# A graph network on one core: how the second layer norm takes its variance, is scaled, turned and stored

## What is computed

```python
# x: 50000 x 64; W: 8 relations x 64 x 64; rel: the relation of each edge
xw = jnp.einsum('ni,rih->rnh', x, W)
transformed = xw[rel, src]
x = _layernorm(x + segment_sum(transformed, dst, 50000))

def _layernorm(x, axis=-1, eps=1e-05):
    m = jnp.mean(x, axis=axis, keepdims=True)
    v = jnp.var(x, axis=axis, keepdims=True)
    return (x - m) / jnp.sqrt(v + eps)
```

## Time and profile before

| | |
|---|---|
| median of 3 runs | 4799.02 us (4790.83 to 4802.06) |
| the profiled execution | 4836.87 us, its span 4835.2 us |
| TensorE matmul busy | 3475.6 us, 72% of the span |
| GpSimd (POOL) busy | 2850.0 us, 59% |
| VectorE (DVE) busy | 2155.2 us, 45% |
| ScalarE (ACT) busy | 1390.9 us, 29% |
| mean granted TensorE clock | 0.703 |
| DMA | 589.50 MB, mean 122 GB/s over the span |

### The profile page before, as it was taken

How to read it: one execution, slowest core, us unless ns; L and a number is a source line. 1 busy time by engine, 2 the same in 40 slices (tenths; PEclk the granted TensorE clock), 3 DMA queues, 4 the chain that set the end, 5 groups by cost and what they waited for, 6 DMA issues and landing times. The chain is left out here.

```text
span 4835.2 us, 72365 instructions
## 1 busy us (share of the span) xinstructions
PE 3475.6 (72%) x19803; PEld 2837.2 (59%) x19803; DVE 2155.2 (45%) x5433; ACT 1390.9 (29%) x3272; POOL 2850.0 (59%) x2834
## 2 busy tenths in 40 slices
PE   4665537766777537776677998779977777777778
PEld 3342127766333236675577667767746677766778
DVE  8999923342899412223322223424542222622225
ACT  1110002222455401112222564434432222222235
POOL 1778867775677767775577660001127776277753
PEclk9776755555799855555688999989985555755559
DMA  4002312112688731112665785545652111311115
GB/s 132 3 3 80 125 32 55 53 48 76 225 330 329 265 128 27 27 27 98 227 178 153 250 255 174 184 167 203 233 193 86 27 27 25 125 27 27 27 39 185
DMA packets 311487, 589.50 MB, mean 122 GB/s; under 512 B 178785, under 2 KB 180702, under 8 KB 292960
## 3 DMA queue, kind: packets, MB, share of 16 engines
q1 hardware_dynamic: 146819, 465.93, 27.1%
q0 software_dynamic: 87808, 66.01, 6.6%
q10 hardware_dynamic: 76506, 53.12, 3.4%
HBM read 286.68 MB, written 310.95 MB: 124 GB/s over the span
## 5 line engine op out<-in xcount | busy, mean ns | idle before, releaser
L1286 PE MATMUL e_ring<-e_msgs,e_hot 128*128 x6272 | 1387.7, 422 | 574.7 <-DVEq L1158 574.7
L1286 PEld LDWEIGHTS e_ring<-e_msgs,e_hot 128*128 128x128 f32 x6272 | 1352.1, 332 | 611.9 <-issue 611.9
L1035 POOL DMA_INDIRECT e_msgs<-y,index_D x784 | 740.0, 944 | 341.1 <-issue 220.9
L1150 DVE TENSOR_TENSOR e_hot<-e_nodes,keys_D 128x2048 f32<-128x2048 f32 x147 | 336.8, 2291 | 1107.3 <-SPq L1074 1087.0
L611 POOL DMA_INDIRECT list_S<-s_place,s_target x392 | 439.8, 1122 | 216.2 <-issue 119.2
L611 POOL DMA_INDIRECT list_D<-d_place,d_target x392 | 385.5, 983 | 161.5 <-issue 119.0
L1593 POOL DMA_INDIRECT m_far<-x,index_S x392 | 382.5, 976 | 154.1 <-issue 114.3
L1035 POOL DMA_INDIRECT e_msgs<-y,index_S x392 | 386.8, 987 | 135.3 <-issue 117.4
L1035 POOL DMA_INDIRECT e_msgs<-x_by_relation,index_D x392 | 373.0, 951 | 134.7 <-issue 109.1
L2441 POOL TENSOR_TENSOR n_sq<-n_cent 128x1792 f32<-128x1792 f32 x14 | 44.4, 3173 | 671.9 <-DVE n_cent L2336 671.9
L1384 ACT ACTIVATE rows_late<-e_ring,dinv 128x64 f32<-128x64 f32 x784 | 171.5, 330 | 757.0 <-PE e_ring L1286 757.0
(11 more groups left out here) (395 smaller groups left out, 5453.9 us busy)
## 6 DMA issues: line engine op xcount, KB each, us to landing
x_by_relation<-d_stage SPq DMA_DIRECT2D x98, 1024.0 KB, 5.3
m_keyrow<-keys_by_step SPq DMA_DIRECT2D x49, 512.0 KB, 4.6
rows<-pairs_by_edge SPq DMA_DIRECT2D x49, 512.0 KB, 4.7
messages<-rows SPq DMA_DIRECT2D x98, 256.0 KB
rows<-messages SPq DMA_DIRECT2D x49, 512.0 KB, 4.2
sums<-m_stage ACTq DMA_DIRECT2D x98, 256.0 KB, 3.6
n_in<-sums SPq DMA_DIRECT2D x14, 1792.0 KB, 8.2
s_xc<-x_padded SPq DMA_DIRECT2D x28, 448.0 KB, 3.7
```

The source lines that it names most:

```text
L1035: pool.indirect_dma_start(out=msgs[:, (i % HELD) * D:(i % HELD + 1) * D], out_offset=None, in_=source, in_offset=bass.IndirectOffsetOnAxis ...
L1150: nc.vector.tensor_tensor(hot[g % 2][:, :, :], bc(nodes[:, 0:P].unsqueeze(1), [P, GS, P]), bc(order["keys"][:, g * GS:(g + 1) * GS].unsque ...
L1286: mm = nc.tensor.matmul(ring[:, bass.ds(bucket, D)], hot[g % 2][:, k, :], msgs[:, bass.ds(tile, D)], start=False, stop=False, skip_group_c ...
```

## The change

Only the part of `stair_pass` under `normed` changes, that is pass `e1`.

- The sums of squares are taken bank by bank while the edges are still being added: after ScalarE has copied bank m out and refilled the ring, it runs eight `Square` activations of 128x64, each with `accum_out` into one column of `var`, now 128x392. The squares themselves go to `blank` and are not read. VectorE's reductions are gone.
- Behind the last bank there is one root over 128x392 on ScalarE and one reciprocal over 128x392 on VectorE.
- The scaling goes bank by bank: banks m with m % 5 of 0 or 2 (20 of them) on POOL, the other 29 on VectorE.
- TensorE turns a whole bank (four transposes) at a time into one of three PSUM banks; ScalarE alone copies them out, 512 values at a time, into `flat_t`, now a ring of 16 banks in `msgs`.
- SP stores groups of four banks (1 MB), in 13 groups: `x2` when the four banks are scaled, then `x2_turned` when they are turned. The last group has one bank.

```diff
+            def by_pool(m):
+                return m % 5 in (0, 2)
+
+            def wait_normed(eng, count):
+                eng.wait_ge(s_norm_pool, sum(by_pool(m) for m in range(count)))
+                if count > 1:
+                    eng.wait_ge(s_norm_dve, sum(not by_pool(m) for m in range(count)))
+
+            def normalize(on, m):
+                return on.tensor_tensor(of_nodes(bank(m)), of_nodes(bank(m)),
+                                        bc(rstd[:, m * BL:(m + 1) * BL].unsqueeze(2), [P, BL, D]), ALU.mult)
+
+            def flat_t(m, count=1):
+                return msgs[:, m % (TBUFS * TBANKS) * 512:(m % (TBUFS * TBANKS) + count) * 512]
...
@@ POOL
             if normed is not None:
-                for c in range(CHUNKS):
-                    pool.wait_ge(s_rstd, c + 1)
-                    nc.gpsimd.tensor_tensor(nodes_of(rows[:, c * CW:(c + 1) * CW]), nodes_of(rows[:, c * CW:(c + 1) * CW]),
-                                            bc(rstd[c % 2][:, :].unsqueeze(2), [P, CH, D]), ALU.mult
-                                            ).then_inc(s_norm, 1)
+                pool.wait_ge(s_rstd, 1)
+                for m in range(BANKS):
+                    if by_pool(m):
+                        normalize(nc.gpsimd, m).then_inc(s_norm_pool, 1)
...
@@ SP
+                starts = range(0, BANKS, TBANKS)
+                for n, m in enumerate(starts):
+                    count = min(TBANKS, BANKS - m)
+                    wait_normed(sp, m + count)
+                    sp.dma_start(x_out[:, m * 512:(m + count) * 512], bank(m, count)).then_inc(s_xout, 16)
+                    sp.wait_ge(s_turn, m + count)
+                    sp.dma_start(x_turned[:, m * 512:(m + count) * 512], flat_t(m, count)).then_inc(s_tout[n % TBUFS], 16)
+                sp.wait_ge(s_xout, 16 * len(starts))
+                for h in range(TBUFS):
+                    sp.wait_ge(s_tout[h], 16 * len(starts[h::TBUFS]))
...
@@ VectorE
+                dve.wait_ge(s_std, 1)
+                nc.vector.reciprocal(rstd[:, :], std[:, :]).then_inc(s_rstd, 1)
+                dve.wait_ge(s_rstd, 1)
+                for m in range(BANKS):
+                    if not by_pool(m):
+                        normalize(nc.vector, m).then_inc(s_norm_dve, 1)
...
@@ TensorE
+                for m in range(BANKS):
+                    wait_normed(pe, m + 1)
+                    if m >= len(spare):
+                        pe.wait_ge(s_turn, m - len(spare) + 1)
+                    for j in range(BL // 2):
+                        mm = flip128(nc, spare[m % len(spare)][:, j * P:(j + 1) * P], bank(m)[:, j * P:(j + 1) * P],
+                                     K["ident"][:, :])
+                    mm.then_inc(s_pturn, 1)
...
@@ ScalarE, in the loop over the banks, behind begin_bank
+                if normed is not None:
+                    if m >= 1:
+                        act.wait_ge(s_sq, BL * m)
+                    for k in range(BL):
+                        t = m * BL + k
+                        nc.scalar.activation(blank[:, k * D:(k + 1) * D], rows[:, t * D:(t + 1) * D], ACT.Square,
+                                             accum_out=var[:, t:t + 1]).then_inc(s_sq, 1)
...
@@ ScalarE, behind the loop
+                act.wait_ge(s_sq, T)
+                nc.scalar.activation(std[:, :], var[:, :], ACT.Sqrt, scale=1.0 / D, bias=K["eps"][:, 0:1]
+                                     ).then_inc(s_std, 1)
+                act.wait_ge(s_group, GROUPS)
+                for m in range(BANKS):
+                    act.wait_ge(s_pturn, m + 1)
+                    if m % TBANKS == 0 and m >= TBUFS * TBANKS:
+                        act.wait_ge(s_tout[m // TBANKS % TBUFS], 16 * (m // TBANKS // TBUFS))
+                    nc.scalar.copy(flat_t(m), spare[m % len(spare)][:, :]).then_inc(s_turn, 1)
```

More of the change, by code:

```diff
@@ L68 @@
 PIECE = 4
+TBANKS = 4
+TBUFS = 4
 def bc(ap, shape):
@@ L996, in stair_pass @@
             x_out, x_turned = (table.rearrange("(p t) f -> p (t f)", p=P) for table in normed)
[L998 to L1007, removed]
+            var = sb("var", [P, T])
+            std = sb("std", [P, T])
+            rstd = sb("rstd", [P, T])
             s_sq = sem("sq")
-            s_var = sem("var")
             s_std = sem("std")
             s_rstd = sem("rstd")
-            s_norm = sem("norm")
+            s_norm_pool = sem("norm_pool")
+            s_norm_dve = sem("norm_dve")
             s_pturn = sem("pturn")
             s_turn = sem("turn")
-            s_odd = sem("odd")
-            def odd_before(k):
-                return k // NQ * ODD + k % NQ // 2
             s_xout = sem("xout")
-            s_tout = [sem(f"tout{h}") for h in range(2)]
-            def nodes_of(ap):
-                return ap.rearrange("p (t f) -> p t f", f=D)
+            s_tout = [sem(f"tout{h}") for h in range(TBUFS)]
+            def by_pool(m):
[9 more added lines that the diff above has]
+                return msgs[:, m % (TBUFS * TBANKS) * 512:(m % (TBUFS * TBANKS) + count) * 512]
         @block.gpsimd
```

## The result

| | before | after |
|---|---|---|
| median of 20 runs | 4799.69 us | 4767.73 us |
| lowest to highest | 4790.83 to 4847.91 | 4761.25 to 4813.07 |
| ratio | | 0.993, 95% interval 0.9901 to 0.9959 |
| profiled execution, its span | 4835.2 us | 4759.5 us |
| norm stretch: last copy out of PSUM to the next pass's first load | 109.2 us | 77.3 us |

The medians differ by 32.0 us, the norm stretches of the two profiled executions by 31.9. The two spans differ by 75.7, and the rest of that is not the change's: of before's 20 runs 14 lie around 4797.4 us and 6 around 4840.8, of after's 15 around 4766.0 and 5 around 4808.9, and the profile of before is one of the long ones, that of after one of the short. The place is an early stage, the scatter of the sorted list, which both kernels run with the same code (before, then after; columns as in the earlier trace rows).

The account below looks back on a forecast made before the run. The old norm stretch was bound by handshakes, the new one by transfers: first store at 2256.0, last 24.64 MB in 60.4 us to 2321.3, next pass 3.7 us later, saving 30.3 us: 4769 us, range 4758 to 4786.

Parts of the forecast that it names:

- What bounds before: Norm stretch before the change, 109.2 us: bound by handshakes around a ring of two chunks, no engine the limit.
- The transfers: Stores of the norm stretch: 25.69 MB at 408 GB/s, 63.0 us, the longest of the four things running side by side.
- Squares beside the gathers: ScalarE in the gather pass: 3.3 us more a bank, 161 us for 49, costing the path nothing except for the last bank.
- The head: Last group's end at 2246.1 to first store at 2256.0: squares 3.3 us, root 0.529, reciprocal 2.60; costs what the old one did.
- Scaling by two engines: Scaling on POOL and VectorE: 20.8 us side by side or 41.7 excluding one another, changing the answer by about 1 us.
- The turning: TensorE's four transposes a bank in the norm stretch: 1.07 us with the wait, 52 us in all, under the transfers.
- The sum: Norm stretch: next pass starts at 2325.0 instead of 2355.3, saving 30.3 us.
- From profile to median: Whole kernel: profiled execution stands 37.9 us above the median; saving carried over unchanged, 4799.0 - 30 = 4769 us.
- B: Stores of the norm stretch: a long stream is slower than bursts, 366 GB/s, saving 23 us, 4776 us; chance 0.15.
- C: Norm stretch: the turning's cadence binds, saving 20 us at 1.5 us a bank, 10 at 1.7; 4779 to 4789 us; chance 0.10.
- D: Norm stretch: three PSUM banks buy no overlap, 1.94 us a bank in series, no change, 4798 us; chance 0.05.
- E: Gather pass: ScalarE becomes the limit if a square takes over 1.1 us; at 1.5 us 4925 us, slower; chance 0.05.

Follow-up runs that it names:

- short_head: VectorE alone scaling, reciprocal cut into groups of four banks, against the kernel with VectorE alone scaling (norm stretch 76.3 us): norm stretch 74.05 us.
- one_bank: One PSUM bank for the turns instead of three, against the changed kernel (norm stretch 77.3 us): norm stretch 105.4 us.
- third_store: One more store of the scaled rows, 12.85 MB to a table nobody reads, against the changed kernel (norm stretch 77.3 us): norm stretch 107.1 us.
- two_banks: Two PSUM banks for the turns instead of three, against the changed kernel (norm stretch 77.3 us): norm stretch 77.4 us.

## Why the prediction was right, point by point

- **What bounds before.** Right that no engine was the limit but a loop over two chunks. One reading in it was wrong: the reciprocal at 2327.79 is not of the chunk that VectorE reduced at 2325.85 but of the one before, whose place in VectorE's order is behind the next reduction. The loop can be followed in the trace of before, with the same steps as in the earlier trace rows one chunk earlier:

```profile
2317.05 1.70 ACT L1472 ACTIVATE e_msgs<-rows 128x1792 f32<-128x1792 f32 x1
2320.72 0.32 DVE L1237 RECIPROCAL e_rstd<-e_std 128x28 f32<-128x28 f32 x1
...
2324.36 1.12 PE L82 MATMUL e_spare<-ident,rows 128*128 128x128 f32 x4 [0.54 <-POOL rows L1048]
...
2330.93 0.37 ACT L1487 COPY e_hot<-e_spare 128x256 f32<-128x256 f32 x1 [0.89 <-PE e_spare L82]
2331.19 1.70 ACT L1472 ACTIVATE e_msgs<-rows 128x1792 f32<-128x1792 f32 x1
```

  A square, its reduction (2318.78), the reciprocal of the chunk before, POOL's scaling of it (2321.11), its turn and the copies out, and only behind the last copy, in ScalarE's order, the next square but one: 14.14 us for two chunks, 7.07 each, while the stores run beside it. The change takes the sums out of this loop, and what is left of the stretch is filled by full-rate stores.
- **The transfers.** Right. The 408 GB/s came out as 415, so 25.69 MB are 61.9 us for a forecast of 63.0.
- **Squares beside the gathers.** Right that they are free; no copy out came later. Their price was too high: a bank took 2.02 us (2205.17 to 2207.19) instead of 3.3. The row used was an activation that reads PSUM and takes its scale from memory (0.330 us); the square reads SBUF and has no such scale, and takes 0.24 (which of the two differences it is was not tried), and the separate read of the accumulator, 0.19 by the profile and not the 0.08 of VectorE's, overlaps the squares beside it, so that the two together come to 0.25 a node.
- **The head.** 9.0 us against 9.9, the sum of the cheaper squares (1.3 less), a root at 0.62 instead of 0.53, the reciprocal exactly at its row, 2.60, and the first four banks scaled and their store issued in 3.07 instead of 2.8. `short_head` shows that a shorter reciprocal counts one for one.
- **Scaling by two engines.** The prediction left open whether they exclude one another and said it would not change the sum by more than 1 us. The profiles bear both out: in company they need 4.9 us more than VectorE alone, and the kernel gains 1.0 us by leaving POOL out. The Trainium skill, "SBUF — State Buffer", section "Who interferes with whom", calls it an exclusive lock. The trace agrees in kind; in size the 34.5 us measured are less than the 29 x 0.60 + 20 x 1.0 = 37.5 of turns taken in full.
- **The turning.** Mis-sized without effect: 1.07 us a bank at the lower clock level was assumed, 52 in all, but the granted clock rose to 1.00 in the first part, and all transposes together were busy 30.7 us (at 0.50, in `one_bank`, 1.09 a bank or 53). That it had no effect is no merit of the price: anything under the 62 us of stores would have done. For the same reason "the new wait on `s_tout` doesn't bite" failed: ScalarE waited 17.7 us for turned buffers. It was harmless, as the same sentence says for the higher clock, since those are the binding stores. SP, too, ran ahead: the `x` stores were issued 2.9 to 4.4 us apart until 2244.57 and 4.5 to 5.3 from there on, not 5.1 throughout, and landed some 15 us after their issue.
- **The sum.** Next pass 77.3 us after the last copy out, forecast 78.9; saved 31.9 against 30.3; median 4767.7 against 4769.
- **From profile to median.** Right to carry the saving over as it stands. The 37.9 us by which the profiled execution stood above the median lie far from the change: its slow scatters alone take 44 us more than those of the short runs profiled, and the other stages vary by some us in either direction.
- **Rivals.** B (slower long streams): refuted, 415 GB/s over 53 us and 419 over 80 us in `third_store`. With it goes, for this kernel on one core, the figure of about 358 GB/s that the prediction took from the Trainium skill, "DMA: Bandwidth & Descriptors", section "Where 436 GB/s comes from". C: refuted by `two_banks` and `third_store`. D gave 1.94 us a bank for a serial round, and `one_bank`, made to be serial, took 1.85; the changed kernel isn't serial. E: the accumulating square costs about 0.25 us apiece, far from the 1.1 at which ScalarE would have set the pace.

## What to carry to other kernels

When a reduction must be complete before a normalization can start, take it piece by piece under the stage that makes the data, and then ask the same of everything behind it: here the change as a whole brought 32 us, and moving the scaling, the turn and the stores as well brought 61 more. Before giving work to a second engine, price the pair together; two engines on banks of the same buffer were slower than the better one alone. And before a difference of two spans is read as a change's effect, compare the stages that the change doesn't touch.

## What was not expected of the hardware

The 392 indirect scatters of the sorted list take 1.01 or 1.12 us apiece in the mean from one profiled execution to the next, with the same code, which is 44 us, more than this change brings. The difference arises only where large transfers run beside them (share 0.45 or 0.43 of the DMA engines from 460 to 500 us): there 40 us hold 25 scatters of 1.38 us or 32 of 0.98. What decides between the two was not tried. VectorE and POOL, both scaling from SBUF, went from 0.679 and 1.042 us to 1.53 and 1.49, and together took 34.5 us for what VectorE alone does in 29.6 and strict turns would do in 37.5; which part of POOL's instruction leaves VectorE free stays open.
